# Edge sums of a graph network kernel: from TensorE sums in the loop to VectorE sums with one TensorE sum behind it

## What is computed

```python
def _mlp(h, W, b, gamma, beta):
    h = h @ W + b
    mu = jnp.mean(h, axis=0)
    var = jnp.var(h, axis=0)
    h = (h - mu) * jax.lax.rsqrt(var + EPS) * gamma + beta
    return h * jax.nn.sigmoid(h)
msg = _mlp(jnp.concatenate([x[row], edge_attr], axis=1), W1, b1, g1, be1)
sums = jax.ops.segment_sum(msg, col, num_segments=N)
```

## Times and profile before

| | us |
|---|---|
| median of 3 runs | 7859.46 (7859.25 to 7867.06) |
| span of the profiled execution | 9014.9 |
| edge pass in it, about | 1848 to 4244 |
| second gather stretch, about | 5008 to 7679 |
| busy in the span: PE, DVE, ACT, POOL | 5434.1, 2921.7, 1301.5, 3562.5 |

### The profile page before, as it was taken

The page is one execution under the profiler, slowest core; times in us unless marked ns, Lnnn a source line. Parts: engine busy times, 40 slices in busy tenths (PEclk is TensorE's granted clock), DMA queues, the critical chain, the costliest instruction groups (busy, mean ns, idle before and its releaser), DMA issues.

```text
span 9014.9 us, 163525 instructions
## 1 busy us (share of the span) xinstructions
PE 5434.1 (60%) x62971; PEld 4715.0 (52%) x62971; DVE 2921.7 (32%) x5181; ACT 1301.5 (14%) x1613; POOL 3562.5 (40%) x3543
## 2 busy tenths in 40 slices
PE   6999889933333333333652455544555455799999
PEld 6999779922222222222542344433444344799998
DVE  6999521111111111112863323332332332311111
ACT  4777510000000000000750000000000000000000
POOL 2111000056666666666725555555555555000000
PEclk9999899966666666666985666666666766899999
DMA  4444268733333332333831222222222222688887
GB/s 129 183 182 182 86 218 254 247 78 81 87 82 81 82 82 76 82 82 98 251 97 35 56 73 73 75 70 70 73 73 74 76 73 76 196 276 268 264 259 229
DMA packets 559779, 1155.29 MB, mean 128 GB/s; under 512 B 155247, under 2 KB 367217, under 8 KB 546465
## 3 DMA queue, kind: packets, MB, share of 16 engines
q1 hardware_dynamic: 234784, 794.54, 27.5%
q10 hardware_dynamic: 215616, 239.17, 8.2%
q0 software_dynamic: 108896, 114.33, 6.5%
HBM read 898.83 MB, written 248.88 MB: 127 GB/s over the span
## 4 chain that ended last, share of the span: by engine, by line
PE 36%; issue 26%; another core or an unknown queue 15%; DVE 5%; ACT 2%; POOL 1%; DVEq 1%; DMA 1%; ACTq 0%; POOLq 0%; SPq 0%; PEldq 0%
PE banks L859 18%; PE banks L953 10%; PE banks L963 5%; POOL gath L366 1%; DVE oneh L1014 1%; DVE area L1836 1%; DVE area L1894 1%; ACT gath L1383 1%; DVE oneh L1845 1%; ACT banks L1380 1%; PE banks L552 1%; PE banks L540 1%; PE banks L1543 1%; PE banks L1552 0%
## 5 line engine op out<-in xcount | busy, mean ns | idle before, releaser
L366 POOL DMA_INDIRECT gath<-tab_l,idx x3328 | 3145.1, 945 | 3296.1 <-DMA idx<-src_idx 1131.6
L1552 PE MATMUL banks<-area,ones 128*128 128x448 f32 (+1 forms) x1040 | 604.9, 752 | 1248.1 <-DVE area L1836 1050.8
L953 PE MATMUL banks<-area 128*128 128x128 f16 x4802 | 575.4, 247 | 894.6 <-issue 893.9
L1552 PEld LDWEIGHTS banks<-area,ones 128*128 128x128 f32 x1040 | 284.5, 285 | 1536.2 <-issue 1522.1
L953 PEld LDWEIGHTS banks<-area 128*128 128x128 fp8e4 x4802 | 356.6, 107 | 1095.2 <-issue 1091.2
L963 PE MATMUL banks<-oneh,gath 128*64 128x128 f32 x3328 | 581.2, 353 | 411.9 <-DMA gath<-tab_l,idx 349.8
L1836 DVE TENSOR_TENSOR area<-gath,banks 128x448 f32<-128x448 f32 (+1 forms) x256 | 138.6, 583 | 1992.2 <-remote 1194.1
L963 PEld LDWEIGHTS banks<-oneh,gath 128*64 128x64 f32 x3328 | 544.7, 188 | 439.0 <-DMA gath<-tab_l,idx 355.6
L825 ACT CAST wide<-banks 128x784 uint16<-128x784 f32 x784 | 651.5, 859 | 221.9 <-PE banks L782 221.9
L794 PE MATMUL banks<-feat,wide 128*128 128x129 f16 x9604 | 670.6, 220 | 0.3 <-ACT wide L825 0.3
L794 PEld LDWEIGHTS banks<-feat,wide 128*128 128x128 fp8e4 x9604 | 606.2, 97 | 0.5 <-issue 0.5
(11 more groups left out here) (257 smaller groups left out, 6169.2 us busy)
## 6 DMA issues: line engine op xcount, KB each, us to landing
gath<-counts SPq DMA_DIRECT2D x294, 784.0 KB, 4.5
oneh<-counts SPq DMA_DIRECT2D x294, 784.0 KB, 4.5
counts<-wide SPq DMA_DIRECT2D x98, 1568.0 KB, 5.2
gath<-counts ACTq DMA_DIRECT2D x98, 784.0 KB
area<-counts ACTq DMA_DIRECT2D x98, 784.0 KB
area<-edge_feat SPq DMA_DIRECT2D x128, 448.0 KB
gath<-tab_l,idx POOLq DMA_INDIRECT x3328
edge_h<-area ACTq DMA_DIRECT2D x128, 416.0 KB
```

What stands on the lines that cost most here:

```text
L366: pool.indirect_dma_start(out=to[:, h, c, 0:H], out_offset=None, in_=table[:, :], in_offset=bass.IndirectOffsetOnAxis(ap=idx[:, slot, c:c ...
L953: last = T.matmul(to, part_in[u].bitcast(f8)[:, t, s * P:(s + 1) * P], block_rows[:, k % 2, s, :, :].rearrange("p a f -> p (a f)"), start= ...
L1552: ins = T.matmul(bank[n][:, 0:(hi - lo) * H], ones[:, :], src[:, lo:hi, :].rearrange("p c f -> p (c f)"), start=first and lo == 0, stop=la ...
```

## The change

The sums over the partitions leave the loop. `accum` has two halves, one for h and one for the squares; both are cleared before the loop. For each group DVE adds `ebuf` onto the first and `emsg` onto the second (`accumulate`, after the onehots of the same group), and PE adds each half up over the partitions once, behind the loop. `s_eacc` becomes one semaphore, which starts at 2 and which DVE raises once a group.

```diff
-                pe.wait_ge(s_eacc[0], 1)
                 pe.wait_ge(s_pair, 32)
-                pe.sem_inc(s_eacc[1], 2)
-                add_up(4, accum[:, 0, :, :], True, False)
-                add_up(5, accum[:, 0, :, :], True, False)
                 with pe.Fori(0, ITERS) as i:
...
                         last.then_inc(s_emm, 1)
-                    for h in range(2):
-                        hold(pe, s_eh, 2 * i + h + RING + 1)
-                        add_up(4, ebuf[:, h, :, :], False, False)
-                        hold(pe, s_esq, 2 * i + h + 1)
-                        add_up(5, emsg[:, h, :, :], False, False).then_inc(s_eacc[1], 1)
-                add_up(4, accum[:, 0, :, :], False, True)
-                last = add_up(5, accum[:, 0, :, :], False, True)
-                last.then_inc(s_bn, 1)
+                pe.wait_ge(s_eacc, GROUPS + 2)
+                add_up(4, accum[:, 0, :, :])
+                add_up(5, accum[:, 1, :, :]).then_inc(s_bn, 1)
...
-                V.memset(accum[:, 0, :, :], 0.0).then_inc(s_eacc[0], 1)
+                V.memset(accum, 0.0).then_inc(s_eacc, 1)
                 dve.sem_inc(s_eh, RING)
+                dve.sem_inc(s_eacc, 1)
...
+                def accumulate(q, h):
+
+                    hold(dve, s_eacc, q + 2)
+                    hold(dve, s_eh, q + RING + 1)
+                    V.tensor_tensor(accum[:, 0, :, :], accum[:, 0, :, :], ebuf[:, h, :, :], ALU.add)
+                    hold(dve, s_esq, q + 1)
+                    V.tensor_tensor(accum[:, 1, :, :], accum[:, 1, :, :], emsg[:, h, :, :], ALU.add)\
+                        .then_inc(s_eacc, 1)
...
-                        hold(dve, s_eacc[1], q + 1)
+                        hold(dve, s_eacc, q + 1)
...
+                        accumulate(q, h)
```

More of the change, by code:

```diff
@@ L265, in gnn_program @@
         s_esq = sem("edge_squared")
-        s_eacc = sems("edge_accumulated")
+        s_eacc = sem("edge_accumulated")
         s_est = sems("edge_stored")
@@ L1357, in edges_to_sums_act @@
                         hold(act, s_eh, 2 * i + h + RING + 1)
-                        hold(act, s_eacc[1], 2 * i + h + 1)
+                        hold(act, s_eacc, 2 * i + h + 1)
                         S.activation(emsg[:, h, :, :], ebuf[:, h, :, :], ACT.Square).then_inc(s_esq, 1)
@@ L1547, in edges_to_sums_pe, with add_up @@
             def edges_to_sums_pe(early=False):
-                def add_up(n, src, first, last):
+                def add_up(n, src):
                     for lo, hi in ((0, CA), (CA, C)):
@@ L1553, in add_up @@
                                        src[:, lo:hi, :].rearrange("p c f -> p (c f)"),
-                                       start=first and lo == 0, stop=last and hi == C)
+                                       start=lo == 0, stop=hi == C)
                     return ins
```

## The result

| | kernel before | changed kernel |
|---|---|---|
| median of runs, us | 7859.35 (7853.27 to 7867.06, 4 runs) | 7956.74 (7954.15 to 7957.85, 4 runs) |
| ratio | | 1.0121 (95%: 1.0107 to 1.0136) |
| span of the profiled execution, us | 9014.9 | 7954.1 |

The change costs 97 us; 85 were forecast. The profiled execution of the changed kernel took 7955.88 us, as long as its other runs. The one of the kernel before did not, so the two spans can't be compared. A second profile of the kernel before, taken as the first experiment, spans 7865.6 us, and the stages are compared with that one.

A forecast was written before the change was run, and what follows sets the result against it. The prediction took POOL's nearly unbroken gathers as the bound. Blocked gathers (83 us) plus 2 us behind the loop, with 0 for removing PE's sums, gave 7859.5 + 85 = 7945 us, +1.1%; 8-in-10 range 7858 to 8080.

The forecast's parts named there:

- One in which POOL issues gathers nearly without a break: Run without recording: POOL's gathers set the pace, 16.2 us a group; PE and DVE edge work counts only where stopping gathers.
- Rival 2: Edge pass: waits behind PE's sums are real, so removing them saves 319 less 83 us; 7624 us, chance 0.10.
- The removal is worth 0, hidden by POOL: Edge loop: PE's column sums, 5.9 us a group, are covered by POOL's gathering, so removing them gains 0.
- Two adds at 1.02, 1.97 together: DVE in each group: an add takes 1.02 us; two, overlapping by 0.07, occupy 1.97.
- 0.65 us a group x 128 = 83: Edge pass: DVE's adds with two SBUF operands block gathers, 0.65 us in each of 128 groups, 83 us.
- (a): Group outcome: the gather starting 0.08 us behind the first add wins; the next is blocked by the second, 0.52 us.
- (b): Group outcome: the gather is blocked by the first add and slips in between the adds, 0.81 us.
- A gather slips in between the adds: Edge pass: a gather blocked by the first add starts before the second, not after both; 0.81 us a group.
- rival 1: Edge pass: the lock is held over both adds, about 1.6 us x 128 = 205 us; 8065 us, chance 0.20.
- Rival 3: Edge pass: adds miss gather starts or delays fall into POOL's existing waits; 0 to 15 us, 7862 us, chance 0.12.
- +2 behind the loop: Behind the loop: onehots, two adds and 8 matmul records end 2 us later than PE's former 16 records.
- The sum: Whole kernel: 83 us in the gathers plus 2 behind the loop, 85 us slower, 7945 us.

The follow-up runs named there:

- experiment 2: TensorE's half of the change alone: against the kernel before, PE's sums leave the loop and DVE adds nothing; 7875.26 us, ratio 1.0016.
- experiment 3: As experiment 2, with a wait and 14 one-column matmuls put into PE's program ahead of the edge loop; 7864.61 us, ratio 0.9998.
- experiment 4: DVE's adds alone: the changed kernel with PE's sums kept in its loop; 7954.81 us, ratio 1.0114.
- experiment 7: The changed kernel with the two adds moved ahead of the onehots of the same group; 7890.25 us, ratio 1.0033.
- experiment 8: As experiment 7, with a wait and 14 one-column matmuls ahead of the edge loop in PE's program; 7877.79 us, ratio 1.0011.
- experiment 6: The changed kernel with one add instead of two: only the squares are accumulated; 7945.37 us, ratio 1.0101.
- experiment 5: The changed kernel with a wait and 14 one-column matmuls ahead of the edge loop in PE's program; 7952.83 us, ratio 1.0109.
- the filler: A wait and 14 one-column matmuls put into PE's program ahead of the edge loop; first in experiment 3, 7864.61 us.

## Why the prediction was right

- **"One in which POOL issues gathers nearly without a break."** Right: 2077.0 us and 0.3 us of waits in the second profile. The prediction came to it by setting the span against the runs and asking which stages could hold the difference, with the waits of the earlier trace rows speaking the other way. Two details were off. It gave the stretch from 5008 to 7679 all 1664 gathers, though the earlier trace rows count 1501 in it; so its excess was not 594 us, and the two gather stretches could hold not 913 us but the whole 1148 that the second profile shows. And the 1155 us do not come from recording as such: the second profile and that of the changed kernel are as long as their runs. Only that one recording was long, and why is open. Rival 2 (7624) took these waits at their word; the edge pass without the sums is 2076.7 us.
- **The removal is worth 0, hidden by POOL.** Right in the loop (experiments 2 to 4). PE's products even grew to 423 ns, from 274 in the second profile, as the granted clock of the stretch went from 0.66 to 0.53. It is hidden just as well: DVE waited for a product once, for 3.3 us. Not foreseen: cutting PE's program cost 10 us in the last stage of experiment 2, and put 7.3 us of gaps into the changed kernel's, whose last stage was still only 2.2 us longer.
- **Two adds at 1.02, 1.97 together.** Right: 1868.72 to 1870.67 is 1.95.
- **0.65 us a group x 128 = 83.** Measured 0.70 and 89.2, of which the held gathers are 0.67 and 85.4. The rule, rest of the add less 0.13, held for all 127 lengthened gathers to within 0.01 us. I had taken a value between outcomes (a) and (b); it was (b) nearly always. Its forecast size, 0.81, was for a gather 0.08 us behind the add; the median was 0.18. That 0.65 came so near is therefore in part luck: counting in (a) took off about as much as the later start of the gathers did. The gathers start 0.01 to 0.35 us into the add, over the whole pass, and a mean over that spread is a better estimate than one group.
- **A gather slips in between the adds.** Right, against rival 1 (8065): no gather was held over both, the longest took 1.78 us. The Trainium skill (SBUF — State Buffer, section "SBUF: two separate sides") calls the port pair an exclusive lock that whichever starts first keeps for its whole instruction. The trace agrees for an add that starts first, and it adds that between two queued adds a waiting gather gets the pair. It disagrees for a gather that starts first: the add beside it takes 1.01 to 1.06 us, where the rule would have it wait for the gather's end, 0.8 us in experiment 4.
- **Rival 3 (no change).** Its condition, adds that miss the starts, is what experiments 7 and 8 nearly bring about by position: a sixth of the cost.
- **+2 behind the loop.** The eight matmuls took 5.91, not half of sixteen, as assumed. Against the first profile the step is 11.07 - 9.12 = 1.95 us, against the second 11.07 - 9.88 = 1.2: nearer to +2 than to 0, and small beside the 10 us by which the medians of one kernel differ.
- **The sum.** 85 forecast, 97 by the medians, 88.5 by the two profiles. Of the 12 us between 85 and 97, 6 are the edge pass's gathers (89 against 83; 2 of them held ones, 4 the slightly longer mean of all others). The other 6 us are within what the medians of the kernel before vary from one set of runs to another (7859.35 to 7869.23).

## What to carry to other kernels

Before moving work onto an engine with idle time, look at what shares a port with it: here the adds' two SBUF inputs cost POOL 89 us while DVE was 71% idle in the edge pass, and adds of the same size with one operand in PSUM cost POOL nothing. Where a short instruction repeats at a fixed phase against another engine's instructions, its cost is a matter of that phase: the same adds cost about 0.7 or 0.12 us a group by their place in the program. And when a recorded span stands 15% above the runs, first find out which stages the excess is in, or profile again, before believing any wait.

## What was not expected of the hardware

- An add that starts while a gather runs (0.13 us in, experiment 4, or 0.52, experiment 7) or together with it (experiment 6) loses 0 to 0.07 us, and the gather nothing; one that starts 0.07 us ahead of a gather costs it 0.8 us. Who is first decides, but the two don't pay alike. The border is sharp: in the changed kernel and experiments 4, 5 and 6 taken together, all 45 gathers that start 0 to 0.031 us behind an add keep their length, and all 475 that start 0.034 us or more behind it, with over 0.3 us of the add left, are held. A short lead is in the changed kernel's first group:

```profile
1851.88 1.01 DVE L1824 TENSOR_TENSOR area<-area 128x832 f32<-128x832 f32 x1
1851.95 1.76 POOL L366 DMA_INDIRECT gath<-tab_l,idx  x1 [0.30 <-issue]
```
- Taking instructions out of TensorE's program ahead of one loop put a second stop of about 1.3 us behind each of six returns of a later loop. All five kernels with the shorter program show it (7.3 to 8.0 us in sum), none of those with the filler or with the sums kept. That it hangs on what stands ahead of the loop in PE's program is shown; what in the chip makes it so is not. Nor do these gaps account for the last stage's length: it exceeds the second profile's by 2.2 us in the changed kernel and by 9.2 to 14.8 us in the four others.
- One profile of a kernel can be 15% longer than the next (9014.9 and 7865.6 us) and show hundreds of microseconds of semaphore waits that the other lacks. All of the excess stood in the two stretches in which POOL gathers.
